# First chunk of a layernorm, ffn and attention kernel: issuing queue, identity products and key layout

## What is computed

```
x = x + 0.5 * ffn(layernorm(x))                 # ffn(z) = z W^T + b + (z V_r) C^T
x = x + attention(layernorm(x))                 # 16 heads of 16, causal
x = x + 0.5 * ffn(layernorm(x))                 # the same weights

att  = (q k^T) / sqrt(16)                       # per head, causal
att  = ((att*att + 1) if att > 0 else (1 - att/100)) / 1000      # no softmax; 0 below -100
y    = (att v) @ W_proj
```

## Time and profile before

| | |
|---|---|
| median of 3 runs | 1689.58 us (1689.31 to 1691.23) |
| the profiled execution, own time | 1690.41 us |
| its span, first to last instruction | 1688.6 us |
| mean granted TensorE clock | 0.988 |
| busy: TensorE, ScalarE, VectorE, GpSimd | 94%, 81%, 79%, 74% |
| DMA | 206.16 MB, mean 122 GB/s |

### The profile page before, as it was taken

The page is one execution under the profiler, slowest core; times in us unless marked ns, Lnnn a source line. Parts: engine busy times, 40 slices in busy tenths (PEclk is TensorE's granted clock), DMA queues, the critical chain, the costliest instruction groups (busy, mean ns, idle before and its releaser), DMA issues.

```text
span 1688.6 us, 67714 instructions
## 1 busy us (share of the span) xinstructions
PE 1593.2 (94%) x27238; PEld 826.6 (49%) x27238; DVE 1332.2 (79%) x3281; ACT 1369.2 (81%) x2182; POOL 1246.8 (74%) x1314
## 2 busy tenths in 40 slices
PE   8788999999999999999999999999999899999997
PEld 6444544444455545444455554544445554444443
DVE  5678787878787787878878688787978768888885
ACT  3467879888987988888887888888888689788884
POOL 3577777877788786876868887786778778667663
PEclk9899999999999999999999999999999999999999
DMA  3655553334345444442435543334433545323311
GB/s 118 183 166 144 147 149 102 105 96 127 99 124 170 137 143 120 127 119 83 121 107 171 164 141 115 98 121 120 135 102 104 166 132 155 109 82 87 88 51 56
DMA packets 183381, 206.16 MB, mean 122 GB/s; under 512 B 27164, under 2 KB 157076, under 8 KB 181276
## 3 DMA queue, kind: packets, MB, share of 16 engines
q1 hardware_dynamic: 183068, 201.77, 40.7%
HBM read 123.26 MB, written 76.30 MB: 118 GB/s over the span
## 4 chain that ended last, share of the span: by engine, by line
PE 70%; DVE 16%; ACT 7%; issue 4%; POOL 3%; DMA 0%; SPq 0%; ACTq 0%; POOLq 0%; DVEq 0%
PE y_ps L1306 27%; PE score L1306 22%; PE bank L1306 18%; DVE rp L1230 10%; PE bank L1345 3%; ACT rp L1104 3%; DVE lin L1236 2%; ACT rp L1124 2%; DVE bnst_ln L1255 1%; ACT rp L1120 1%; POOL rp L996 1%; POOL z L956 1%; PE bank L1389 1%; DVE st_add L1216 1%; ACT parts L1084 0%
## 5 line engine op out<-in xcount | busy, mean ns | idle before, releaser
L1230 DVE TENSOR_SCALAR rp<-score 128x512 f32<-128x512 f32 (+3 forms) x1728 | 964.7, 585 | 254.8 <-PE score L1306 250.2
L996 POOL TENSOR_TENSOR rp<-rp 128x1024 f32<-128x1024 f32 (+3 forms) x416 | 723.4, 1747 | 96.2 <-DVE rp L1230 84.8
L1306 PE MATMUL score<-qs,ks 96*32 96x512 bf16 (+3 forms) x10240 | 720.2, 350 | 55.1 <-DVE lin L1236 29.6
L1306 PE MATMUL y_ps<-rp,vt 128*16 128x512 f32 (+3 forms) x5120 | 594.5, 532 | 12.1 <-ACT rp L1120 4.6
L1104 ACT ACTIVATE rp<-score 128x512 f32<-128x512 f32 (+3 forms) x832 | 439.7, 569 | 191.5 <-PE score L1306 187.8
L1306 PEld LDWEIGHTS score<-qs,ks 96*32 96x32 bf16 x10240 | 297.5, 96 | 428.9 <-DVE rp L1230 188.2
L1120 ACT ACTIVATE rp<-rp,rise 128x1024 f32<-128x1024 f32 (+3 forms) x416 | 443.5, 1095 | 4.2 <-POOL rp L971 4.1
L971 POOL TENSOR_SCALAR_AFFINE_SELECT rp<-rp 128x256 f32<-128x256 f32 (+1 forms) x384 | 184.6, 481 | 235.2 <-ACT rp L1104 151.2
L1124 ACT ACTIVATE rp<-rp 128x2048 f32<-128x2048 f32 (+2 forms) x224 | 328.9, 1468 | 3.4 <-POOL rp L971 3.1
L1236 DVE SCALAR_TENSOR_TENSOR lin<-score,slope_mask 128x128 f32<-128x128 f32 x768 | 214.0, 279 | 0.1
L1306 PEld LDWEIGHTS y_ps<-rp,vt 128*16 128x16 f32 x5120 | 138.5, 96 | 103.6 <-issue 19.7
(11 more groups left out here) (96 smaller groups left out, 1274.8 us busy)
## 6 DMA issues: line engine op xcount, KB each, us to landing
ks<-part_scratch SPq DMA_DIRECT2D x648, 64.0 KB, 2.4
qs<-part_scratch SPq DMA_DIRECT2D x384, 64.0 KB, 2.4
part_scratch<-parts SPq DMA_DIRECT2D x14, 1536.0 KB, 6.0
vt<-v_scratch SPq DMA_DIRECT2D x102, 128.0 KB, 2.7
state_scratch<-st_new SPq DMA_DIRECT2D x16, 528.0 KB
x_sb<-in_L_attn_x_dram SPq DMA_DIRECT2D x16, 512.0 KB, 4.5
x_scratch<-x SPq DMA_DIRECT2D x16, 512.0 KB, 5.4
qT_scratch<-qkT SPq DMA_DIRECT2D x16, 512.0 KB, 3.5
```

Source lines behind the costliest of these rows:

```text
L996: pool.tensor_tensor(half, half, half, ALU.mult).then_inc(squared["pool"], 1)
L1230: nc.vector.tensor_scalar(rp[T % RP_BUFS][:, 2 * u + v, off:CH], score[H % S_BUFS][:, v, off:CH], 0.0, RISE, ALU.max, ALU.add).then_inc(ra ...
L1306: return nc.tensor.matmul(*args, start=start, stop=stop, skip_group_check=True)
```

## The change

For the first chunk (0) and the first sequence's chunks (0 to 3) it does this:

- `B_FIRST` puts kT half 0 right behind qT half 0, then k half 0, qT half 1, kT half 1, k half 1. kT of chunk 0 is made by strips of products of w_qkv with z2T (as qT is), not by transposes of k_sb. k is still made.
- ScalarE issues `first qT` (3 transfers), chunk 0's `first v` (4), and the stores of qT and v to DRAM of chunks 0 to 3. For chunk 0 the qT ones stand between ScalarE's two copies of chunk 1's z1T banks, the v ones a slot behind its second v copy.
- Two of the four blocks of chunk 0's ln2 z are made by ScalarE, with a semaphore of their own.
- GpSimd's three memsets wait until vr is centred.
- `weights()` makes vr times cT as one product 256 columns wide and adds the two w_in products to it.
- `BUSY` goes from (12, 4, 4, 20) to (9, 4, 4, 18). New identity products stand in front of score halves below H32: two each before H0 to H6, none before H7, H8, H15, H16, H23, H24 and H31, one each before the others, 32 in all. They write the accumulator that no visit uses at the time, and wait for y_copied of the visit before.

```diff
-B_FIRST = {"qT": (0, 12), "k": (2, 6), "kT": (10, 14), "v": (17, 20), "state": (24, 25, 26, 27)}
+B_FIRST = {"qT": (0, 8), "kT": (3, 10), "k": (4, 11), "v": (17, 20), "state": (24, 25, 26, 27)}
-BUSY = (12, 4, 4, 20)
+BUSY_HALVES = 2 * QUADS * NB
+BUSY = (9, 4, 4, 18)
+SENT_BY_ACT = CPB
...
                 if (x.kind, x.i) == ("qT", 1):
-                    put(x.empty_at + (1 if x.chunk else 16), "qT", x.chunk)
+                    if x.chunk >= SENT_BY_ACT:
+                        put(x.empty_at + 1, "qT", x.chunk)
...
-                if (x.kind, x.chunk, x.i) == ("qT", 0, 1):
-                    put(x.empty_at + 9, "first qT")
...
-                    if (x.kind, x.i) == ("v", 1):
+                    if (x.kind, x.i) == ("v", 1) and x.chunk > 0:
                         put(x.empty_at + 1, "first v", x.chunk)
                     if (x.kind, x.i) == ("state", NB - 1):
-                        put(x.empty_at + (7 if x.chunk else 2), "first st", x.chunk)
+                        put(x.empty_at + (7 if x.chunk else 10), "first st", x.chunk)
...
+            pool.wait_ge(vr_centred, 3)
             pool.memset(k_sb[:], 1.0).then_inc(filled, 1)
...
+                last = NB - 1 if chunk else NB // 2 - 1
+                if i <= last:
+                    ins = pool.tensor_scalar(z[:, i, :], x1[:, i, :], rstd["ln2"][:, i:i + 1], shift[:, i:i + 1],
+                                             ALU.mult, ALU.add)
+                if i == last:
                     ins.then_inc(z_ready, 1)
...
+            def send(kind, a):
+                wait_emptied(act, kind, a, 1)
+                if kind == "qT":
+                    if a == 0:
+                        for g in range(1, QUADS):
+                            cols = slice(CH * g, CH * g + CH)
+                            act.dma_start(qT[1:QD + 1, cols], qkT[(g % 2) * QD:(g % 2) * QD + QD, g // 2, :]).then_inc(qT_loaded[g], 16)
+                    act.dma_start(qT_d[a].rearrange("k p t -> p k t"), qkT[:, 0:KC, :]).then_inc(qT_stored, 16)
+                if kind == "v":
+                    if a == 0:
+                        for x in [x for x in KEY_LOADS if made_here(x) and x.kc == 0]:
+                            act.dma_start(vt[:, NB * x.place:NB * x.place + NB, :], v_sb[:, x.g, :, :]).then_inc(v_loaded[x.place], 16)
+                    act.dma_start(v_d[a], v_sb[:]).then_inc(v_stored, 16)
...
+                sent_at.setdefault(o.place["qT", a, 1].empty_at + (6 if a == 0 else 1), []).append(("qT", a))
+                sent_at.setdefault(o.place["v", a, 1].empty_at + 1, []).append(("v", a))
...
+                    if step == SCALES and k == "ln2" and chunk == 0:
+                        act.wait_ge(norm_ready, 1)
+                        for i in range(NB // 2, NB):
+                            ins = nc.scalar.activation(z[:, i, :], x1[:, i, :], ACT.Identity, bias=shift[:, i:i + 1],
+                                                       scale=rstd["ln2"][:, i:i + 1])
+                        ins.then_inc(first_z_ready, 1)
...
                 for k in range(KC):
+                    mm(y_ps[k][:, 0:DM], vrT[:, P * k:P * k + P], cT, start=True, stop=False)
                     for j in range(KC):
-                        dst = y_ps[k][:, P * j:P * j + P]
-                        mm(dst, w_in[:, j, P * k:P * k + P], ident[:], start=True, stop=False)
-                        ins = mm(dst, vrT[:, P * k:P * k + P], cT[:, P * j:P * j + P], start=False, stop=True)
+                        ins = mm(y_ps[k][:, P * j:P * j + P], w_in[:, j, P * k:P * k + P], ident[:], start=False, stop=j == KC - 1)
...
-                if kind == "kT":
+                if kind == "kT" and a == 0:
+                    wait_emptied(pe, "z2T", a, 1)
+                    for kc in range(KC):
+                        ins = strips(dst[:], w_qkv[:, kc, DM + P * i:DM + P * i + P], z2T[:, kc, :], start=kc == 0, stop=kc == KC - 1)
+                elif kind == "kT":
...
+                last = (H + 1) // 2 - LAG - 1
+                if H < BUSY_HALVES and (last < 0 or last > VISIT_FIRST[WORK[last][0]]):
+                    visit = WORK[max(last, 0)][0]
+                    if visit > 0:
+                        pe.wait_ge(y_copied, visit)
+                    for _ in range(2 if H < 8 else 1):
+                        mm(y_ps[(visit + 1) % 2][:, 0:P], ident[:], ident[:])
```

More of the change, by code:

```diff
@@ L491, in build @@
         z_ready = sem("z_ready")
+        first_z_ready = sem("first_z_ready")
         w_centred = sem("w_centred")
@@ L707, in _ @@
                 if (x.kind, x.i) == ("qT", 1):
-                    put(x.empty_at + (1 if x.chunk else 16), "qT", x.chunk)
+                    if x.chunk >= SENT_BY_ACT:
+                        put(x.empty_at + 1, "qT", x.chunk)
                     there["qT", x.chunk] = x.empty_at + 1 + LANDED
                 if (x.kind, x.i) == ("v", 1):
-                    put(x.empty_at + (1 if x.chunk else 24), "v", x.chunk)
+                    if x.chunk >= SENT_BY_ACT:
+                        put(x.empty_at + 1, "v", x.chunk)
                     there["v", x.chunk] = x.empty_at + 1 + LANDED
@@ L828, in slot @@
                             sp.dma_start(vt[:, NB * x.place:NB * x.place + NB, :], v_sb[:, x.g, :, :]).then_inc(v_loaded[x.place], 16)
-                    if what == "first qT":
-                        wait_emptied(sp, "qT", 0, 1)
-                        for g in range(1, QUADS):
-                            cols = slice(CH * g, CH * g + CH)
-                            sp.dma_start(qT[1:QD + 1, cols], qkT[(g % 2) * QD:(g % 2) * QD + QD, g // 2, :]).then_inc(qT_loaded[g], 16)
                     if what == "first st":
@@ L955, in normalise @@
                         pool.wait_ge(job_done, o.made("z2T", chunk - 1, 1))
-                ins = pool.tensor_scalar(z[:, i, :], x1[:, i, :], rstd["ln2"][:, i:i + 1], shift[:, i:i + 1],
-                                         ALU.mult, ALU.add)
-                if i == NB - 1:
+                last = NB - 1 if chunk else NB // 2 - 1
[3 more added lines that the diff above has]
+                if i == last:
                     ins.then_inc(z_ready, 1)
@@ L1090, in copy_y @@
                 nc.scalar.activation(y_sb[w % 2][:], y_ps[w % 2][:], ACT.Copy).then_inc(y_copied, 1)
+            sent_at = {}
+            for a in range(SENT_BY_ACT):
+                sent_at.setdefault(o.place["qT", a, 1].empty_at + (6 if a == 0 else 1), []).append(("qT", a))
+                sent_at.setdefault(o.place["v", a, 1].empty_at + 1, []).append(("v", a))
             def slot(s):
@@ L1095, in slot @@
                         empty(x)
+                for kind, a in sent_at.get(s, ()):
+                    send(kind, a)
                 H = o.halves.get(s)
@@ L1170, in aggregate @@
                     dve.wait_ge(z_ready, chunk)
+                    dve.wait_ge(first_z_ready, 1)
                 for i in range(NB):
@@ L1361, in job @@
                             keep_busy(BUSY[3])
+                            pe.wait_ge(first_z_ready, 1)
                         pe.wait_ge(z_ready, a + 1)
```

## The result

The changed kernel takes 1695.79 us (median of 7 runs, 1694.22 to 1699.31), beside 1689.53 us for the kernel before in the same session. The ratio is 1.0034, 95% interval 1.0024 to 1.0045: slower by about 5.7 us. I had forecast 1684.2 and a range up to 1690.0, so both sign and range were wrong. The profiled execution took 1696.64 us, with a mean granted clock of 0.992 (0.988 before).

A forecast was written before the change was run, and what follows sets the result against it. TensorE, 94% busy, was taken as the bound, with the first 160 us open to gain. 4.25 - 0.65 + 2.2 - 0.7 + 1.1 - 0.8 = 5.4 us off 1690.41, less 0.83, gave 1684.2 us; range 1680.3 to 1690.0.

The forecast's parts named there:

- (a) to (d): Start to z transposes: opening products 0.7, `weights()` 0.75, first ffn 1.7, z split 1.1; 4.25 us gained.
- (b): `weights()` at the start: fewer records and weight-shape alternations, 2.6 us long, 0.75 us gained, bounds 0 and 1.5.
- (e): Keys, order and ScalarE's transfers: 0.65 us lost at chunk 1's ffn, bounds 0 and 3.1.
- (f): Two products each before H0 to H6, 0.47 us, covered by waits for VectorE: no loss.
- (g): Clock from 55.7 to 68.9 us: half clock becomes full, 2.2 us gained, bounds 0 and 2.4.
- (h): The full stretch to 90 us: three more products cost 0.7 us.
- (i): Clock from 93.0 to 99.6 us: 1.1 us gained, between 0 and 2.2.
- (j): Twelve products before H17 to H30, 2.8 us at 0.236 each: 0.8 us on the path, bounds 0 and 2.8.
- Rival three: Identity products at H9 to H30 become the cost, 8.2 us where the clock stays low: 1695.5 us; chance 0.08.
- Rival two: ScalarE's issues go at half SP's pace while SP loads keys, costing 3.1 us: 1686.6 us; chance 0.09.
- Rival one: Clock does not hold behind `weights()` or from 55.7 us on, 0.4 us gain left: 1689.2 us; chance 0.20.
- Rival four: Early start is eaten later by a clock fall in a new place: 1687 us; chance 0.06.

The follow-up runs named there:

- e9: The kernel of e3 run again (SP issues all transfers, no identity products before score halves): 0.9976 of the kernel before, 1685.51 us.
- e3: The changed kernel with all ScalarE's transfers back on SP and no identity products before score halves: 0.9980 of the kernel before, 1686.41 us.
- e14: The changed kernel without identity products before score halves, only qT's transfers on ScalarE, v's back on SP: 1.0004 of the kernel before.
- e13: The changed kernel without identity products before score halves, only v's transfers on ScalarE, qT's back on SP: 0.9984 of the kernel before.
- e10: The changed kernel with transfers on SP and only the 14 products before H0 to H6: 0.9984 of the kernel before, 1687.35 us.
- e2: The changed kernel with all of ScalarE's transfers back in SP's queue, identity products kept: 1.0012 of the kernel before, 1692.93 us.
- e6: The changed kernel with only the 14 identity products before H0 to H6, the 18 later ones left out: 1.0011 of the kernel before.
- e1: The changed kernel without the 32 identity products before score halves: 0.9995 of the kernel before, 1689.99 us.
- e4: The kernel before with only the start's edits (memsets' wait, `weights()`, split z, product counts), no new keys: 0.9986, 1689.13 us.
- e5: The changed kernel run again on another chip: 1.0045 of the kernel before, 1697.86 us.
- e11: The kernel of e1 with ScalarE's vt and v transfers nine slots later; vt still went out at 40.31 us as before; no overall time given.

## Why the prediction was wrong

(a) to (d), **the start: right, and a little small.** I gave 4.25 us and z transposes at 21.2; the changed kernel has them at 20.31, other runs of the same start at 20.3 to 21.5. `weights()` took the forecast 2.6 us and the ffn the forecast 3.66, at full clock. By the rule of the Trainium skill ("TensorE: Matmul & The Clock Gate", Part 3, "The mechanism") that I weighed in (b), that a weight load overlaps running products only when its row group differs, my estimate was 2.9 us; the measured 2.6 speaks for the row of 0.118 us a product. The lead of 4.7 us at the first y copy of e9 and e3 (4.67 and 4.83) is what remained of it without the rest of the change, about what 0.9976 and 0.9980 give at the end.

(e) **ScalarE's transfers: the step that failed first.** The part that I priced came true: an issue takes ScalarE 0.61 to 0.84 us, and chunk 1's ffn began at 41.80, where the lead had shrunk by 0.93 us (I said 0.65). What I wrote on the transfers themselves, that they "gain nothing, since no score waited for a DMA", looked only at who waits for them, not at what they wait beside. The Trainium skill, "DMA: Bandwidth & Descriptors", section "Issuing engines are not separate DMA queues", says that transfers run on the same 16 engines and interleave whichever engine starts them. The traces agree: the key loads took 2.8 us beside an idle ScalarE queue and 4.7 beside its transfers. In SP's single file the same transfers left room, and TensorE's instructions came in time. The bound of 3.1 us that I gave to this step held no such case: in the changed kernel the hole and the clock behind it cost 5.2 us (8.64 for this ffn against 3.48), in e14 against e13 the medians differ by 3.4, with the wait for zT.

(f) **The first 14 products: right at 0.** e10 against e9, 8.67 against 8.66 us.

(g) **2.2 us from the clock at 55.7 to 68.9: failed.** The clock was better, but full where TensorE waits for VectorE and GpSimd, and low again behind 60 us: the first y copy is 0.17 us earlier in e10, most of it there before. I took "z of chunk 1 sets the time up to 62.86" rightly, and did not ask that the gaps ahead of it, with no product in them (3.07 us in the changed kernel), would lower the clock once more.

(h), (i), (j) **the later 18 products: the largest error.** I had them at 0.7 in (g), 0.7 in (h) and 0.8 in (j), less 1.1 of clock in (i): 1.1 us on the path. e2 against e10 gives 0.28%, 4.7 us; e6 against the change 0.23%, 3.9 us (less clean, as the hole was 0.60 us in e6's trace and 2.75 in the change's). The first term that was mis-sized is the price of 0.236 us: I took it from a run of like products. Here a product of 128x128 weights stands mostly between strips of 32, the step is then 0.42 us, and six of them cost 2.23 us between the first two y copies, 0.37 each. I had used this very thing in (b), where each alternation cost 0.18 us extra, 0.236 + 0.18 = 0.42, and left it out in (h) and (j). The second is the share of (j) on the path, 0.8 of 2.8: 18 at 0.37 are 6.7 us, and 4.7 were lost with the clock's gain taken off, so most of them lay on it. The profile before had also shown the stretch up to 90 us at 98% busy. The clock gain of (i) is real (1.00 in place of 0.50) and smaller than the price.

**Together:** on one chip, e3 (neither) is at 0.9980, ScalarE's transfers alone (e1) at 0.9995, the products alone (e2) at 1.0012. The two steps, 0.15 and 0.32%, add up to 1.0027 for both; the two measurements of the change are 1.0034 and 1.0045, with intervals that reach down to 1.0024. So the parts are about additive, and no large one is missing.

**Two slips in my sums.** Rival three takes its 0.4 us off twice; its own terms give 1695.9, not 1695.5. And the terms named for the lower end of the forecast's own range give 1681.6, not 1680.5. Neither changes the outcome.

**The rivals.** Rival three gave 1695.5 us, and 1695.79 was measured, but the near match is luck, and it is only half right: the place (H9 to H30) and the sign are, its mechanism was a product of 0.457 us at the low clock, where it was one of 0.42 at the full one, about 4.7 us in all instead of 8.2; the hole, which it didn't have, is in the measured time too. I gave it 0.08. Rival two's condition, issues at half pace, did not come true. Rival one's low clock held in part. Rival four, an early start that is eaten later, is next.

**An early start is not kept whole.** I took all later waits as fixed. The 64 copies of y (one a visit) are the marks. In e9 the lead was 4.67 us at the first copy and 1.8 at the fourth (122 us), where e10's stayed at 4.9. From the seventh copy (195 us) to 490 us the distance to the profiled execution of before keeps within 0.2 us in 13 of the 15 other traces (0.5 in e4 and e13); near 500, 920 and 1330 us, where the short visits of a new sequence begin, it jumps by up to 5 us either way. The windows of 920 to 930 us, the kernel before and then the changed one:

```profile
920.00:930.00 10.00, 9.60 (x200) 6.26 (x196) 6.87 (x24) 9.19 (x17) 8.10 (x13) 1.00 0.48 125
```

```profile
920.00:930.00 10.00, 7.22 (x122) 5.62 (x112) 4.90 (x21) 3.37 (x8) 6.22 (x9) 0.67 0.48 134
```

TensorE in the changed kernel shows what came ahead of the low clock:

```profile
924.34 0.41 PE L1341 MATMUL y_ps<-qT,st 66*16 66x128 f32 x3 [2.78 <-issue]
```

It is the same kind of stop, and the clock is at 0.50 from 925 to 930 us behind it. In the 16 traces TensorE has 66 stops of more than 0.5 us behind the first 20 us that no semaphore ends. All of them stand at a border of 256 records as above (one is a record off), and all end 2.2 to 3.2 us after a q8 transfer is seen. The kernel before has them too: 1.49 us at 109.75, 1.81 at 517.3 and 2.90 at 1323.0. Which border is hit differs from trace to trace. So the changed kernel lost 4.7 us near 920 by two stops and the clock (3.7 behind at 551 us, 8.4 at 952). At 1320 to 1330 it was the kernel before whose clock fell further (0.66 against 0.98), and 2.2 us came back. e5, the same kernel, shows both as well, e1 the first not. This scatter of about 4 us is why each verdict rests on 5 to 12 executions, and why the profile of a single one tells the order of events but not the total. It also answers rival four: what eats an early start in these traces, or gives it back, is where the instruction transfers fall beside bursts of other ones.

**What stays open.** That the instruction transfer waits behind other transfers was argued from its being 3.5 to 5.7 us late where the DMA engines are full and in time where they are not; no run delayed it by itself. Why it was 3.5 us late in e1 and 5.2 in e11, whose TensorE has the same list of instructions, isn't known; the hole's length follows from it (0.60 and 2.41 us). e4, whose TensorE has another list of instructions (kT by transposes), seems to break the rule, with a transfer at 40.55, 1.5 us late and 1.2 us ahead of its ffn, and no hole. But its block begins at 43.50, in the middle of the ffn and 2.95 us behind the transfer, so it fits. How the loss in the median divides between holes in front of 50 us and stops further on was not measured.

## What to carry to other kernels

Before transfers are spread over two issuing engines, look at what the DMA engines are doing in that stretch, and not only at who waits for the transfers: here one queue in single file kept bursts apart, and instructions travel beside the data. When an engine stops with no semaphore to blame, look at the instruction queue of the profile, and at whether the stops stand a fixed number of records apart. A filler product is free only in front of a wait that is longer than it, and its price is the step between the starts of its neighbours, with the change of weight shape in it, not its own length. And a higher clock is worth something only where the engine has work from end to end, so ask of each stretch who sets its time before counting on it.

## What the runs showed of the hardware

- An engine can stop inside an accumulation with no semaphore involved: 0.60 to 2.75 us behind the 12th record of 64, ending 2.7 to 3.1 us after a transfer of 16 KB on the instruction queue was seen.
- TensorE took one such transfer for 256 of its records. All 66 stops over 0.5 us with no semaphore stood at a border of 256 records (0.5 to 3.6 us, also in the kernel before), and no block began less than 2.16 us after its transfer was seen.
- VectorE's centring of a 128x256 tile took 1.06 us an instruction beside a GpSimd memset and 0.30 without it.
- The same 64 KB key loads landed in 2.3 to 2.8 us from one queue and in 4.7 to 5.0 beside a second; four transfers of 128 KB in 2.6 and 8.3.
- One float32 128x128 product between strips of 32 columns cost 0.42 us (0.37 on average over six places), a second behind it 0.22.
